# Three edges of a decoder kernel: output stored by group, a TensorE loop written out, a last group written on its own

## The reference, cut to what matters

```python
# layer 2, "attn": a state-space block, forward (m1) and on the reversed sequence (m2), 16 states
x = x + _L2_attn_ref(_layernorm(x), m1_in_w, ..., m2_in_w, ...)
# layer 3, "attn": 32 query heads, 16 key/value heads, 64 wide, causal, with a linear bias
scores = jnp.einsum('bhqd,bhkd->bhqk', q, k) / math.sqrt(64) + bias[None]
attn = jax.nn.softmax(jnp.where(causal, scores, -inf), axis=-1)
x = x + (jnp.einsum('bhqk,bhkd->bhqd', attn, v) @ W_out)
# layer 3, "ffn": 8 experts, the best two weighted by the router
h = silu(einsum('td,edf->etf', flat, w1)); y = einsum('etf,efd->etd', h, w2)
x = x + einsum('etd,te->td', y, cw)
```

## Time and profile before

| | |
|---|---|
| median of 3 runs | 7244.17 us (7243.53 to 7258.09) |
| profiled execution: its own time | 7231.49 us |
| profiled execution: span, first to last instruction | 7229.6 us |
| busy share PE / DVE / ACT / POOL | 89% / 74% / 56% / 39% |
| mean granted clock of PE, of full speed | 0.962 |
| `mamba` second half and end | to about 4117 us |
| `a3` | about 5190 to 6390 us |
| `topk_ffn` | about 6723 to 7212 us |

### The profile page before, as it was taken

One profiled execution on the slowest core, in us unless ns is written; L12 is line 12 of the kernel. 1 busy time (PEld: TensorE's weight loads), 2 busy tenths in 40 slices (PEclk: granted clock), 3 DMA queues, 4 the chain that ended last, 5 costly groups with the idle time before them and its releaser, 6 DMA issues. The chain is left out here.

```text
span 7229.6 us, 188705 instructions
## 1 busy us (share of the span) xinstructions
PE 6436.1 (89%) x74428; PEld 3944.6 (55%) x74428; DVE 5332.4 (74%) x8931; ACT 4057.1 (56%) x6024; POOL 2813.5 (39%) x1680
## 2 busy tenths in 40 slices
PE   7989987887797999989999789999899999989998
PEld 5767665444532333333333256666576767666676
DVE  7867576665467999999999856687577777768444
ACT  4556343665447777777777745455344444456433
POOL 3311175332216888888888501164022222221000
PEclk9999988999798999999999899999999999999999
DMA  1000000000101222222222100000000000000000
GB/s 29 0 21 12 8 6 8 3 4 2 15 0 62 76 78 76 80 75 76 73 76 75 47 12 14 22 17 3 12 2 2 2 2 2 2 16 14 1 0 23
DMA packets 115879, 190.00 MB, mean 26 GB/s; under 512 B 38661, under 2 KB 74746, under 8 KB 114970
## 3 DMA queue, kind: packets, MB, share of 16 engines
q1 hardware_dynamic: 112218, 183.47, 8.0%
q10 hardware_dynamic: 3264, 0.54, 0.1%
HBM read 173.87 MB, written 7.98 MB: 25 GB/s over the span
## 5 line engine op out<-in xcount | busy, mean ns | idle before, releaser
L2611 POOL TENSOR_TENSOR m_dBx<-m_dtx,m_Bs 128x1024 f32<-128x1024 f32 x515 | 1166.5, 2284 | 227.1 <-DVE m_hs L2976 185.0
L2976 DVE TENSOR_TENSOR_SCAN m_hs<-m_ps_dA,m_dBx 128x512 f32<-128x512 f32 x1030 | 1203.0, 1212 | 56.6 <-POOL m_dBx L2611 56.0
L2730 PE MATMUL m_ps_y<-m_yc,ident 128*128 128x512 f32 x2060 | 1021.4, 618 | 0.0
L2835 ACT ACTIVATE m_ps_dA<-m_dt,m_A 128x504 f32<-128x504 f32 x1030 | 683.3, 679 | 426.0 <-DVE m_hs L2976 423.4
L2107 POOL TENSOR_TENSOR a_s<-a_s,a_den 128x1024 f32<-128x1024 f32 x128 | 243.8, 1904 | 1123.7 <-DVE a_den L2153 1123.7
L2987 DVE TENSOR_TENSOR m_yc<-m_hs,m_ps_C 128x1024 f32<-128x1024 f32 x515 | 619.3, 1203 | 1.2 <-PE m_ps_C L2711 1.1
L2730 PEld LDWEIGHTS m_ps_y<-m_yc,ident 128*128 128x128 f32 x2060 | 350.0, 189 | 357.2 <-issue 357.2
L2711 PEld LDWEIGHTS m_ps_C<-m_parts,m_sel 48*128 48x128 bf16 x516 | 47.7, 92 | 567.7 <-DVE m_yc L2987 421.4
L2711 PE MATMUL m_ps_C<-m_parts,m_sel 48*128 48x512 bf16 x516 | 199.7, 387 | 176.4 <-DVE m_yc L2987 176.2
L636 POOL TENSOR_TENSOR c_kbd<-c_kf,c_hmask 128x1024 f32<-128x1024 f32 x66 | 125.1, 1895 | 503.0 <-ACT c_kf L545 484.9
L2151 DVE TENSOR_REDUCE a_den<-a_s 128x16 f32<-128x1024 f32 x128 | 156.1, 1219 | 207.5 <-ACT a_s L2058 207.5
(11 more groups left out here) (750 smaller groups left out, 15803.9 us busy)
## 6 DMA issues: line engine op xcount, KB each, us to landing
m_Bs<-BC_rows SPq DMA_DIRECT2D x258, 512.0 KB, 3.6
c_kvb<-in_ctxT SPq DMA_DIRECT2D x68, 128.0 KB, 2.1
c_kvb<-in_ctxT SPq DMA_DIRECT2D x17, 256.0 KB, 2.7
out_dram<-X SPq DMA_DIRECT2D x1, 4096.0 KB
BC_rows<-m_low SPq DMA_DIRECT2D x33, 64.0 KB, 2.9
part_rows<-m_split SPq DMA_DIRECT2D x33, 48.0 KB, 1.7
m_parts<-part_rows SPq DMA_DIRECT2D x33, 48.0 KB, 1.7
m_piece<-BC_rows SPq DMA_DIRECT2D x33, 32.0 KB, 1.7
```

Of the source, the lines that this page charges most:

```text
L2611: return nc.gpsimd.tensor_tensor(to, one, other, ALU.mult)
L2730: last = nc.tensor.matmul(ps_y[:, m, :], C.ident[:], of[:, m, :], start=s == 0, stop=s == NS - 1)
L2835: nc.scalar.activation(seqs(ps_dA[:, h % 3, :]), seqs(dt[:, par, m, :]), ACT.Exp, scale=A[:, second, m, s:s + 1]).then_inc(decay, 1)
L2976: nc.vector.tensor_tensor_scan(hs[:, s % HS, m, :], ps_dA[:, (2 * s + m) % 3, :], dBx[:, s % BX, m, :], 0.0, ALU.mult, ALU.add).then_inc(s ...
```

## The change

1. `store_x` is gone. `topk_ffn` gets a list for SP that stores each group's 256 KB as soon as `out_read` says that its rows are final.
2. In `attn64`, PE's passes 1 to 7 are written out where `HG` > 1, so in `a3` alone. The other engines keep their loops.
3. In `mamba`, `LOOPS[1]` ends one pair earlier. Group 30 is written out, and group 31 has code of its own without group 32: no `front`, no states 0 to 2, no `split_rows` of it. SP's groups 30 and 31 are written out and its transfers for group 32 go.

```diff
+        @block.sync                                  # topk_ffn
+        def _(sp):
+            out_rows = out.rearrange("(n p) d -> p n d", p=P)
+            for i in range(C.NG):
+                tiles = slice(i * TPG, (i + 1) * TPG)
+                sp.wait_ge(out_read, i * NE + NE + 2)
+                sp.dma_start(out_rows[:, tiles, :], C.X[:, tiles, :]).then_inc(stored, 16)
+            sp.wait_ge(stored, C.NG * 16)
...
-            with pe.Fori(1, C.NG // 2) as i:         # attn64, PE
-                for s in range(NX):
-                    slot(i, s)
+            if HG > 1:
+                for i in range(1, C.NG // 2):
+                    for s in range(NX):
+                        slot(i, s)
+            else:
+                with pe.Fori(1, C.NG // 2) as i:
+                    for s in range(NX):
+                        slot(i, s)
...
-        LOOPS = ((0, C.NG // 2 - 1), (C.NG // 2, C.NG))
+        LOOPS = ((0, C.NG // 2 - 1), (C.NG // 2, C.NG - 1))
...
-            for m in range(NHF):                     # mamba, PE
-                nc.tensor.matmul(ps_y[:, m, :], C.ident[:], yc[:, (AHEAD - 1) % 2, m, :], start=False, stop=True)
+            group(GROUPS - 2, 0, [1, 1, 1, 1], 1)
+            for s in range(AHEAD, NS):
+                if s == SKIPPED:
+                    skip(1, 1)
+                step(GROUPS - 1, s, 1, final=True)
+            project(GROUPS - 1, 1, True)
...
+            def final_group(i, par):                 # mamba, DVE
+                for s in range(AHEAD, NS):
+                    scan(i, s)
+                    weigh(i, s - 1)
+                weigh(i, NS - 1)
+                gated(i, par)
+                add_output(i, True)
...
-            weigh(GROUPS, AHEAD - 1)
+            group(GROUPS - 2, 0, True)
+            final_group(GROUPS - 1, 1)
...
-def store_x(C, out):
-            sp.dma_start(out.rearrange("(n p) d -> p n d", p=P), C.X[:, 0:C.NT, :]).then_inc(stored, 16)
-            sp.wait_ge(stored, 16)
```

More of the change, by code:

```diff
@@ L1615, in topk_loads, with topk_ffn @@
     return loads + [(t["w2"][:, e, :, :], W["w2"][e].rearrange("(c p) d -> p c d", p=P)) for e in range(NE)]
-def topk_ffn(C, name, W):
+def topk_ffn(C, name, W, out):
     nc = C.nc
@@ L1642, in topk_ffn @@
         hid_done, hid_ready, out_done, out_read = (sem(n) for n in ("hid_done", "hid_ready", "out_done", "out_read"))
+        stored = sem("stored")
         scales = NormScales(C, sc, 1e-5)
@@ L2592, in _ @@
                     group(pair * 2 + par, par)
[L2593 to L2596, removed]
+            for par in range(2):
+                group(GROUPS - 2 + par, par)
         n_prepared = 2
@@ L2651, in _, with group @@
                 state(0, s, 0, True)
-            with pool.Fori(0, C.NG) as pair:
-                for par in range(2):
[L2654 to L2659, removed]
+            def group(i, par):
+                for s in range(AHEAD, NS):
+                    state(i, s, par)
+                    front(i + 1, s, 1 - par)
+                for s in range(AHEAD):
+                    state(i + 1, s, 1 - par)
+            with pool.Fori(0, C.NG - 1) as pair:
+                for par in range(2):
+                    group(pair * 2 + par, par)
+            group(GROUPS - 2, 0)
+            for s in range(AHEAD, NS):
+                state(GROUPS - 1, s, 1)
         @block.tensor
@@ L2717, in skip, with project @@
                     nc.tensor.matmul(ps_y[:, m, :], diagD[:, m, :], xs[:, par, m, :], start=False, stop=False)
-            def project(i, second):
+            def project(i, second, final=False):
                 pe.wait_ge(y_ready, i + 2)
-                pe.wait_ge(xs_ready, i * NHF + 5)
+                pe.wait_ge(xs_ready, i * NHF + (3 if final else 5))
                 for p in range(TPG):
@@ L2731, in add, with step @@
                 last.then_inc(y_added, 1)
-            def step(j, s, par, between=None):
+            def step(j, s, par, between=None, final=False):
                 rank = DVE_WEIGHS.index(s)
@@ L2737, in step @@
                     spread_C(j, DVE_WEIGHS[rank + 1], par)
-                else:
+                elif not final:
                     spread_C(j + 1, 0, 1 - par)
@@ L2763, in front, with group @@
                     convolve(j + 1, (s - 12) // 2, (s - 12) % 2)
-            def group(i, par, of):
+            def group(i, par, of, fronts=AHEAD):
                 for s in range(AHEAD, NS):
@@ L2772, in group @@
                 for s in range(AHEAD):
-                    front(i + 2, s, par, True, of[2], of[3])
+                    if s < fronts:
+                        front(i + 2, s, par, True, of[2], of[3])
                     step(i + 1, s, 1 - par, (lambda: project(i, of[0])) if s == 0 else None)
@@ L2793, in _ @@
                     group(pair * 2 + par, par, [1, 1, 1, 1])
-            for m in range(NHF):
-                nc.tensor.matmul(ps_y[:, m, :], C.ident[:], yc[:, (AHEAD - 1) % 2, m, :], start=False, stop=True)
+            group(GROUPS - 2, 0, [1, 1, 1, 1], 1)
+            for s in range(AHEAD, NS):
+                if s == SKIPPED:
+                    skip(1, 1)
+                step(GROUPS - 1, s, 1, final=True)
+            project(GROUPS - 1, 1, True)
         @block.scalar
@@ L2927, in _ @@
                     group(pair * 2 + par, par, [1, 1, 1, 1])
-            front(GROUPS + 1, AHEAD, 1, True, 1, 1)
+            group(GROUPS - 2, 0, [1, 1, 1, 1])
+            for s in range(AHEAD, NS):
+                state(GROUPS - 1, s, 1, 1)
         @block.vector
@@ L3011, in group @@
                 scan(i + 1, 1)
-                dve.wait_ge(y_added, i * NS + NS)
-                nc.vector.tensor_tensor(q[:], sz[:, par, :, :], ps_y[:], ALU.mult).then_inc(y_ready, 1)
+                gated(i, par)
                 weigh(i + 1, 0)
@@ L3016, in group, with gated, add_output @@
                 weigh(i + 1, 1)
+                add_output(i, second)
+            def gated(i, par):
+                dve.wait_ge(y_added, i * NS + NS)
+                nc.vector.tensor_tensor(q[:], sz[:, par, :, :], ps_y[:], ALU.mult).then_inc(y_ready, 1)
+            def add_output(i, second):
                 dve.wait_ge(out_done, i + 1)
@@ L3021, in group @@
                 nc.vector.tensor_tensor(at, ps_j[:].rearrange("p (t d) -> p t d", d=D), at, ALU.add).then_inc(out_read, 1)
+            def final_group(i, par):
+                for s in range(AHEAD, NS):
+                    scan(i, s)
+                    weigh(i, s - 1)
+                weigh(i, NS - 1)
+                gated(i, par)
+                add_output(i, True)
             with dve.Fori(*LOOPS[0]) as pair:
@@ L4237, in both_ways, with last_blocks @@
     mamba(C, "m1", W, BC_rows, part_rows)
-def last_blocks(C, A):
+def last_blocks(C, A, out):
     qkvo = dict(wq="Wq", wk="Wk", wv="Wv", wo="Wo", hmask="hmask")
@@ L4267, in last_blocks @@
         attn16_table(C, "c3", "mask", pick(A, "c3_", bq="bq", bk="bk", bv="bv", bo="bo", table="table3", mask="mask", **qkvo), A["ctxT"])
-        topk_ffn(C, "f3", f3)
+        topk_ffn(C, "f3", f3, out)
 def program(nc, A, out, groups):
@@ L4288, in program @@
                 both_ways(C, ways)
-        last_blocks(C, A)
-        store_x(C, out)
+        last_blocks(C, A, out)
 def kernel(**inputs):
```

## The result

| | before | after |
|---|---|---|
| median | 7243.89 us (7243.53 to 7258.09, 4 runs) | 7198.34 us (7192.73 to 7204.56, 4 runs) |
| profiled execution, span | 7229.6 us | 7198.1 us |
| DVE's last instruction to the end | 17.62 us | 3.23 us |
| gate of group 30 to gate of 31 | 58.05 us | 54.10 us |
| gate of group 31 to the next stage | 15.47 us | 5.04 us |

The changed kernel is faster by 0.7%: ratio 0.9934, 95% interval 0.9919 to 0.9948. The forecast was 7202.1 us. The three edges gave 14.4 + 14.8 + 14.5 = 43.7 us between the two profiled executions (14.8 is the two middle rows, 14.4, and 0.44 more between the gates of groups 29 and 30). Their spans differ by only 31.5 us: the rest of the program took some 12 us longer in this execution, 9.9 of them ahead of the gate of group 0 of the state-space stage (at 2305.79 us in place of 2295.88), where no edit lies.

The account below looks back on a forecast made before the run. PE was taken to bound the kernel, busy for 89% of the span. Gains of 14.0 + 13.6 + 14.5 = 42.1 us took the profiled 7231.49 to 7189.4; adding 12.7 for the median gave 7202.1 us, range 7188 to 7218.

Parts of the forecast that it names:

- Edge 1: The output store behind DVE's last instruction: with fifteen of sixteen stores beside work, a gain of 14.0 us.
- the slower landing of a load: At the output store: a 256 KB load landed in 2.7 us, leaving 4.0 us at the end, a gain of 13.6.
- Rival B: An end moves less than its sum: slow store landing (9.9), state-space lower bound (8.2); 7211.6 us, chance 0.07.
- Edge 2: Last group of the state-space stage: without the work for group 32 the stage ends earlier, a gain of 13.6 us.
- The comparison with groups 14 and 15: State-space stage: these groups, already written out, had gates 58.1 us apart as in the loops, so writing out costs nothing.
- Edge 3: PE's loop in `a3`: writing out its passes removes the added idle time at six jumps back, a gain of 14.5 us.
- the dear jump: Fourth of six jumps in `a3`: 3.97 us more idle, as PE's clock fell to 1.2 GHz for 3.3 us.
- A: Another engine takes over the wait at PE's jumps in `a3`, whose gain is then nothing: 7216.6 us, chance 0.09.
- C: Slower by PE's clock: without pauses in `a3` a lower clock could be granted, 7298 us; chance 0.02.
- D: Straight code is paid after all: about 108 blocks at 0.39 us each eat 42 us, 7244 us; chance 0.02.

## Why the prediction was right, point by point

**The sign, the size and the sum.** Forecast 7202.1 with a range of 7188 to 7218; the three measurements of the changed kernel gave medians of 7198.34, 7194.02 and 7206.27. Three serial pieces were read at their places and added; in the traces each is the same alone and with the others.

**Edge 1: 14.0 forecast, 14.4 found.** The sum by its steps (3.1 us: semaphore, first byte, transfer, end) was nearer than the 14.0 chosen between it and the slower landing of a load; 256 KB landed in 2.3 us. The transfer was the gain, by the run with one store. Rival B fell.

**Edge 2: 13.6 forecast, 14.8 found.** From the gate of group 31 to the next stage the steps gave 5.03 us, and 5.04 were measured. Two steps ahead of it were off. "Writing out groups 30 and 31 costs nothing by itself" missed a gain of 0.44 us for group 30. The comparison with groups 14 and 15 could not show it, as these carry the changeover's work: 63.73 us between the gates of 13 and 14 and 57.96 from 14 to 15 (the prediction says 58.1), and with every loop written out the same two are still 64.93 and 58.18, where all others but one are 57.6. The other step is the latencies taken from the tail, where PE was still in the sum of state 0 when the next row of C was asked for. There the row took 1.24 us and the sum began 1.03 behind its product; here it was 0.57 (4102.58 to 4103.15) and 0.37. The product of state 14 came exactly as reckoned, 48.80 us behind the gate of group 30 (48.79 reckoned). All that is left lies behind it: PE's two sums bind the gate, as reckoned, but 4.1 us behind that product and not 4.9, since they begin 0.66 earlier and last 3.70 in place of 3.85. With 0.44 for group 30 that is the missing 1.2.

**Edge 3: 14.5 forecast and found in the pair of traces, but the term was mis-sized.** The mechanism was right, and so was the cause given for the dear jump ("The fourth cost more because PE's granted clock fell"). What failed is the count: the rows of one execution showed one fall at six jumps, and the sum took it as the rule. The other five traces showed three to five, so the edge is worth some 19.5 us in the mean of six traces, 19.6 by the ratio of the single edge (its interval gives 13 to 27) and 15.1 by its medians. With the mean of 3.3 falls, at the prediction's own prices, it would have been 12.2 + 3.3 x 1.95 = 18.6. The same error stands in the sum a second way: it added the 12.7 us between the profiled execution and the median back in full, though some 4 of them were the loop's own falls, if the executions without a trace fell as often as the traced ones. With 18.6 the sum would have been 7198.0; with all three terms as found (14.4, 14.8 and 19.5) it is 7195.5. The three measured medians spread over 12 us, more than the 4 to 7 us between these sums and 7202.1, so that the forecast lies within about 8 us of each is in part luck.

That a long body is fetched anew and stalls at the jump held: doubling `c2`'s made the stall. The Trainium skill (Runtime: NRT & Kernel Launch, Instruction fetch mechanics) gives PE 128 KiB for code, refilled in 16 KiB blocks, and says that a branch out of the window waits for a fetch; the runs agree in that 4 slots are hardly fetched at all (13 blocks in a stage) and 8 and 16 always are. The 2.04 us that the prediction estimated for a block from the Trainium skill (DMA: Bandwidth & Descriptors, Anatomy of one DMA) stand beside 1.79 us measured at the undisturbed jump in `c2` and 2.03 in `a3`; that section's price is for transfers that GpSimd issues, not for fetches of code, so the nearness shows no mechanism.

**The rivals.** A: no engine took over, and writing out ACT, DVE and POOL there changed nothing. C: the clock did answer, but the other way: it fell at pauses, never in the 1130 us without them. D: PE's code was fetched 18 and 92 times in stretches of 148 and 742 us, where it had been 18 and 99, and `a3` is shorter by just what its jumps had cost, 14.54 us, so that the slots between them are not longer. B: the last store landed in 2.3 us, and edge 2 moved by more than its sum.

## What to carry to other kernels

Read a kernel's serial edges one by one: what runs after the last compute, what the last turn of a skewed loop prepares for nobody, and what each jump back shows as "issue". PE's loop over 4 slots jumped back at no cost, those over 8 and 16 did not; the sign was that PE's instruction fetches went on through the whole stage, and then a jump stalled PE for 2 us and could bring its clock down behind it. A loop can also cost a little all along: those of the state-space stage cost 0.4 us per group. A profile of one execution can miscount what comes by chance (here one fall of the clock at six jumps, where the others had three to five): count such events in several traces before a price is put on them.

## What was not expected of the hardware

Behind idle times of PE of about 2 us its granted clock fell to 1.2 GHz for 3.4 us at 20 of 36 jumps, and each fall cost about 1.8 us more. And an engine that the page shows as 39% busy was still waited for once per group: POOL's hardware loop cost the state-space stage 0.30 us per group of 58, and all engines' loops 0.42. That the registers in its waits make POOL late fits its idle times ("issue" 0.32 against 0.26), but no run takes them apart from the loop.
